# Linear stream of a fused attention and transformer kernel: biases by TensorE, maxima subtracted at eviction, all score products at once in four banks

## The reference

```python
vp = _ln(x, in_ln_w, in_ln_b) @ W_in
v, p = jnp.split(vp, 2, axis=-1)
q = softmax(to_heads(_ln(x, q_ln_w, q_ln_b) @ Wq + bq))
k = softmax(to_heads(_ln(x, k_ln_w, k_ln_b) @ Wk + bk))
k_prev = k shifted by one token
k = (1.0 - smear) * k + smear * k_prev          # smear by head
q, k = q / s, k / s                              # s by head
attn = jnp.tril(jnp.einsum('bhid,bhjd->bhij', q, k) * mask)   # mask: decay by head for 8 heads, ones for 8
norm = 1.0 / (attn.sum(axis=-1) + ATTN_EPS)
o = jnp.einsum('bhij,bhjd->bhid', attn * norm[..., None], v)
out = _ln(jax.nn.silu(p) * o @ W_out, out_ln_w, out_ln_b)
```

## Time and profile before

| | |
|---|---|
| median of 3 runs | 2380.59 us (2374.51 to 2381.43) |
| the profiled execution | 2383.1 us |
| its span | 2381.2 us |
| TensorE busy, products | 2168.9 us |
| TensorE busy, weight loads | 1867.6 us |
| VectorE busy | 1827.8 us |
| ScalarE busy | 1148.8 us |
| GpSimd busy | 934.9 us |
| TensorE's mean granted clock | 0.906 of 2.4 GHz |

### The profile page before, as it was taken

One profiled execution on the slowest core, in us unless ns is written; L12 is line 12 of the kernel. 1 busy time (PEld: TensorE's weight loads), 2 busy tenths in 40 slices (PEclk: granted clock), 3 DMA queues, 4 the chain that ended last, 5 costly groups with the idle time before them and its releaser, 6 DMA issues.

```text
span 2381.2 us, 48786 instructions
## 1 busy us (share of the span) xinstructions
PE 2168.9 (91%) x15282; PEld 1867.6 (78%) x15282; DVE 1827.8 (77%) x5354; ACT 1148.8 (48%) x2734; POOL 934.9 (39%) x941
## 2 busy tenths in 40 slices
PE   4889989999899989999899989989999999999997
PEld 3778877877787877877787877878888888888786
DVE  5667887778767787688767887777888888888885
ACT  2234443344334443344333443346677676776764
POOL 3334453345434453345433453343333333333331
PEclk8778998889978898899888998889999999999999
DMA  4000000000000000000000000012111111111110
GB/s 162 11 13 17 20 18 14 15 19 18 14 13 19 15 18 14 13 21 18 14 13 15 19 18 14 14 51 69 33 36 33 33 37 32 36 33 33 37 33 25
DMA packets 71792, 64.37 MB, mean 27 GB/s; under 512 B 12444, under 2 KB 64984, under 8 KB 71608
## 3 DMA queue, kind: packets, MB, share of 16 engines
q1 hardware_dynamic: 71736, 63.65, 8.9%
HBM read 38.45 MB, written 12.58 MB: 21 GB/s over the span
## 4 chain that ended last, share of the span: by engine, by line
PE 50%; DVE 30%; issue 13%; DMA 3%; ACT 1%; DVEq 1%; SPq 1%; POOL 1%; POOLq 0%; ACTq 0%
PE bank L1327 38%; PE bank L1332 7%; PE bank L1339 5%; DVE prob L940 4%; DVE prob L926 4%; DMA x_shift<-x 2%; DVE rot L1250 2%; DVE sq_sum L1196 2%; DVE qk_sum L1209 2%; DVE rot L1228 1%; DVE hid L1257 1%; DVE v_mix L1223 1%; DVE mix_work L982 1%; DVE h_n L1158 1%; DVE h_n L1156 1%
## 5 line engine op out<-in xcount | busy, mean ns | idle before, releaser
L1327 PE MATMUL bank<-hT_n,w_s 128*128 128x128 f32 x3072 | 389.6, 279 | 0.5 <-ACT hT_n L711 0.5
L1327 PEld LDWEIGHTS bank<-hT_n,w_s 128*128 128x128 f32 x3072 | 364.9, 193 | 15.2 <-issue 10.8
L1332 PE MATMUL bank<-wqkv_s,xT 128*128 128x512 f32 x1152 | 319.4, 413 | 24.0 <-DVE xT L1104 18.4
L741 ACT ACTIVATE prob<-prob,row_min 128x256 f32<-128x256 f32 x512 | 256.1, 503 | 63.8 <-DVE row_min L926 61.5
L1327 PE MATMUL bank<-w_s,hid 128*128 128x256 f32 x768 | 284.5, 489 | 0.2 <-DVE hid L1257 0.2
L1332 PEld LDWEIGHTS bank<-wqkv_s,xT 128*128 128x128 f32 x1152 | 207.8, 192 | 81.8 <-DVE xT L1104 27.1
L711 ACT ACTIVATE k_dec<-bank 128x512 f32<-128x512 f32 x32 | 19.1, 598 | 515.6 <-PE bank L1339 515.6
L940 DVE TENSOR_SCALAR prob<-prob,row_inv 128x256 f32<-128x256 f32 x512 | 224.3, 480 | 9.2 <-DVE row_inv L935 0.2
L926 DVE CUSTOM_DVE_ANT_0 prob<-bank,table,inv_norm 128x256 f32<-128x256 f32 x512 | 226.2, 478 | 2.7 <-issue 2.7
L633 POOL TENSOR_TENSOR rot_other<-raw,rot_t 128x256 f32<-128x256 f32 x256 | 186.5, 761 | 93.3 <-ACT raw L711 93.3
L596 POOL TENSOR_TENSOR inv_norm<-sq_clip,half_neg 128x16 f32<-128x16 f32 x64 | 188.7, 2948 | 63.6 <-DVE sq_clip L1199 63.6
(11 more groups left out here) (182 smaller groups left out, 4699.8 us busy)
## 6 DMA issues: line engine op xcount, KB each, us to landing
k_prev<-k_carry SPq DMA_DIRECT2D x32, 224.0 KB, 2.5
x_s<-in_L_attn_x SPq DMA_DIRECT2D x32, 128.0 KB, 2.1
rot_s<-in_rotary SPq DMA_DIRECT2D x64, 64.0 KB, 2.0
s_between_passes<-s_out SPq DMA_DIRECT2D x32, 128.0 KB, 1.7
x_between_layers<-x SPq DMA_DIRECT2D x32, 128.0 KB, 1.7
x_s<-x_between_layers SPq DMA_DIRECT2D x32, 128.0 KB, 2.0
xn<-x_between_layers SPq DMA_DIRECT2D x32, 128.0 KB, 2.1
s_out<-s_between_passes SPq DMA_DIRECT2D x32, 128.0 KB, 2.1
```

What stands on the lines that cost most here:

```text
L741: ins = act.activation(prob[:, h, :], prob[:, h, :], ACT.Exp, bias=row_min[:, c:c + 1], scale=-1.0, accum_out=row_sum[:, c:c + 1])
L1327: return pe.matmul(out, lhsT, rhs, start=first, stop=last)
L1332: ins = pe.matmul(out, halved(left[:, a]), halved(right[:, b]), start=first and n == 0, stop=last and n == 2)
```

## The change

- The biases of q, k and p are no longer added at eviction. `bias_rows` holds each bias as a high part in row 0 and a low part in row 32, and `pick` has ones in these rows; a first product of 64 rows puts the bias in the bank, and the linear products accumulate on it. v keeps its addition. Setup makes these tiles.
- `less_max`: DVE takes the maxima straight from the bank and subtracts them as it evicts, k first, then q. PE computes k ahead of q. ACT takes the exponential of k and of q by themselves, DVE sums by halves. POOL's subtraction goes.
- tanh reads the bank; the gate is one DVE product, (tanh + 1) times the bank. POOL's two products go.
- All four row groups of the scores are issued in one go, into `mix_bank[0]`, `mix_bank[1]`, `att_bank[0]` and `att_bank[2]`; DVE multiplies all four with the masks, one after the other, ahead of `low_turned` and `residual`. `out_projection` writes `att_bank[1]` in these iterations.
- Order: the key sum (kadd) comes ahead of the rotation products on DVE; the sums of squares (`norms`) come behind the gate; scores b1 come ahead of weighing b0, in all iterations; POOL makes `k_dec` ahead of the inverse norm; PE transposes k and q behind the transposes of b1; two of the second MLP matrix's products come ahead of the output loop, two within it, behind g = 1 and g = 3.

```diff
-        bias_mix = sb("bias_mix", [P, 4, ME])
+        bias_v = sb("bias_v", [P, ME])
+
+        bias_rows, bias_in = sb_halves("bias_rows", [P, 3, ME])
+        pick, pick_in = sb_halves("pick", [P, P])
...
+        score_bank = [mix_bank[0], mix_bank[1], att_bank[0], att_bank[2]]
...
+            pool.memset(pick_in[:, :], 0.0).then_inc(picked, 1)
...
+            pool.memset(pick_in[0:1, :], 1.0).then_inc(picked, 1)
...
-                if mix is not None:
-                    n = mix
-                    pool.wait_ge(mix_dve.sem, mix_dve.at("max", n))
-                    qk_h = qk.rearrange("p (h d) -> p h d", d=MD)
-                    pool.tensor_tensor(qk_h, qk_h, qk_max[:, :].unsqueeze(2).to_broadcast([P, 2 * MH, MD]),
-                                       ALU.subtract).then_inc(mix_pool.done("sub"), 1)
...
-                if proj is not None:
-                    u, p = proj, proj.parity
-                    pool.wait_ge(proj_dve.sem, proj_dve.at("clip", u))
-                    root(inv_norm[:, p, :], sq_clip[:, :], 2 * H).then_inc(proj_pool.done("inv"), 1)
-                if mix is not None:
-                    n = mix
-                    pool.wait_ge(mix_act.sem, mix_act.at("tanh", n))
-                    pool.tensor_tensor(gate[:, :], p_tanh, p_lin, ALU.mult).then_inc(mix_pool.done("gatep"), 1)
-                    pool.wait_ge(mix_pool.sem, mix_pool.at("gatep", n))
-                    pool.tensor_tensor(gate[:, :], gate[:, :], p_lin, ALU.add).then_inc(mix_pool.done("gate"), 1)
...
+                if proj is not None:
+                    u, p = proj, proj.parity
+                    pool.wait_ge(proj_dve.sem, proj_dve.at("clip", u))
+                    root(inv_norm[:, p, :], sq_clip[:, :], 2 * H).then_inc(proj_pool.done("inv"), 1)
+                if mix is not None:
+                    n = mix
...
+                    act.wait_ge(mix_dve.sem, mix_dve.at("ksub", mix))
+                    act.activation(qk[:, ME:2 * ME], qk[:, ME:2 * ME], ACT.Exp).then_inc(mix_act.done("kexp"), 1)
...
+                    act.wait_ge(mix_dve.sem, mix_dve.at("qsub", mix))
+                    act.activation(qk[:, 0:ME], qk[:, 0:ME], ACT.Exp).then_inc(mix_act.done("qexp"), 1)
...
-                    act.wait_ge(mix_pool.sem, mix_pool.at("sub", mix))
-                    act.activation(qk, qk, ACT.Exp).then_inc(mix_act.done("exp"), 1)
...
-                    act.wait_ge(mix_dve.sem, mix_dve.at("p", mix))
-                    act.activation(p_tanh, p_lin, ACT.Tanh, scale=0.5).then_inc(mix_act.done("tanh"), 1)
+                    act.wait_ge(mix_pe.sem, mix_pe.at("p", mix))
+                    act.activation(p_tanh, mix_bank[1][:, :], ACT.Tanh, scale=0.5).then_inc(mix_act.done("tanh"), 1)
...
-                b = mix_bank[r % 2][:, :].rearrange("p (g i) -> p g i", g=MG)
+                b = score_bank[r][:, :].rearrange("p (g i) -> p g i", g=MG)
...
+            def less_max(mix, name, b, at):
+
+                rows = qk_max[:, at * MH:(at + 1) * MH]
+                dve.wait_ge(mix_pe.sem, mix_pe.at(name, mix))
+                dve.tensor_reduce(rows, heads(b[:, :]), AX_X, ALU.max).then_inc(mix_dve.done(name + "max"), 1)
+                dve.wait_ge(mix_dve.sem, mix_dve.at(name + "max", mix))
+                dve.tensor_tensor(heads(qk[:, at * ME:(at + 1) * ME]), heads(b[:, :]),
+                                  rows.unsqueeze(2).to_broadcast([P, MH, MD]), ALU.subtract)\
+                   .then_inc(mix_dve.done(name + "sub"), 1)
+
+            def norms(u):
+
+                dve.wait_ge(proj_act.sem, proj_act.at("square", u))
+                dve.tensor_reduce(sq_sum[:, :], rot[:, :].rearrange("p (h d) -> p h d", d=HD), AX_X, ALU.add)\
+                   .then_inc(proj_dve.done("sqsum"), 1)
+                dve.wait_ge(proj_dve.sem, proj_dve.at("sqsum", u))
+                dve.tensor_scalar(sq_clip[:, :], sq_sum[:, :], 1e-24, None, ALU.max)\
+                   .then_inc(proj_dve.done("clip"), 1)
...
+            b_hi = prob[0:64, 0:6, :].rearrange("p h d -> p (h d)").rearrange("p (n e) -> p n e", n=3)
+            dve.tensor_copy(halved(b_hi), bias_in[0:64, :, :]).then_inc(setup_dve.done("bhi"), 1)
+            dve.wait_ge(setup_dve.sem, setup_dve.at("bhi", ONCE))
+            dve.tensor_tensor(halved(bias_rows[32:64, :, :]), bias_in[32:64, :, :], b_hi[32:64], ALU.subtract)\
+               .then_inc(setup_dve.done("blo"), 1)
+            dve.tensor_copy(halved(bias_rows[0:32, :, :]), b_hi[0:32]).then_inc(setup_dve.done("brow"), 1)
+            dve.wait_ge(picked, 3)
+            dve.tensor_copy(halved(pick[:, :]), pick_in[:, :]).then_inc(setup_dve.done("brow2"), 1)
...
+                if mix is not None:
+                    less_max(mix, "k", mix_bank[0], 1)
+                if a is not None:
                     weigh("a0", a)
                 if mix is not None:
-                    dve.wait_ge(mix_pe.sem, mix_pe.at("q", mix))
-                    dve.tensor_tensor(qk[:, 0:ME], mix_bank[0][:, :], bias_mix[:, 2, :], ALU.add)\
-                       .then_inc(mix_dve.done("q"), 1)
+                    less_max(mix, "q", mix_bank[1], 0)
                 if a is not None:
                     weigh("a1", a)
+                if mix is not None:
+                    dve.wait_ge(mix_act.sem, mix_act.at("kexp", mix))
+                    dve.tensor_reduce(qk_sum[:, MH:2 * MH], heads(qk[:, ME:2 * ME]), AX_X, ALU.add)\
+                       .then_inc(mix_dve.done("ksum"), 1)
+                    dve.wait_ge(mix_dve.sem, mix_dve.at("ksum", mix))
+                    dve.reciprocal(k_norm[:, :], qk_sum[:, MH:2 * MH]).then_inc(mix_dve.done("kinv"), 1)
+                    dve.wait_ge(mix_dve.sem, mix_dve.at("kinv", mix))
+                    dve.tensor_tensor(k_smear[:, :], k_norm[:, :], smear_s[:, :], ALU.mult)
+                    dve.tensor_tensor(k_keep[:, :], k_norm[:, :], keep_s[:, :], ALU.mult)\
+                       .then_inc(mix_dve.done("kw"), 1)
+                if a is not None:
+                    scores("b1", a, att_bank[0])
                     weigh("b0", a)
...
-                if mix is not None:
-                    dve.wait_ge(mix_pe.sem, mix_pe.at("k", mix))
-                    dve.tensor_tensor(qk[:, ME:2 * ME], mix_bank[1][:, :], bias_mix[:, 3, :], ALU.add)\
-                       .then_inc(mix_dve.done("k"), 1)
-                    dve.wait_ge(mix_dve.sem, mix_dve.at("k", mix))
-                    dve.tensor_reduce(qk_max[:, :], heads(qk), AX_X, ALU.max).then_inc(mix_dve.done("max"), 1)
...
-                    dve.wait_ge(mix_pe.sem, mix_pe.at("p", mix))
-                    dve.tensor_tensor(p_lin, mix_bank[1][:, :], bias_mix[:, 1, :], ALU.add)\
-                       .then_inc(mix_dve.done("p"), 1)
-                if mix is not None:
-                    dve.wait_ge(mix_act.sem, mix_act.at("exp", mix))
-                    dve.tensor_reduce(qk_sum[:, :], heads(qk), AX_X, ALU.add).then_inc(mix_dve.done("sum"), 1)
...
+                if u is not None and mix is None:
+                    norms(u)
+                if mix is not None:
+                    dve.wait_ge(mix_act.sem, mix_act.at("qexp", mix))
+                    dve.tensor_reduce(qk_sum[:, 0:MH], heads(qk[:, 0:ME]), AX_X, ALU.add)\
+                       .then_inc(mix_dve.done("qsum"), 1)
+                    dve.wait_ge(mix_dve.sem, mix_dve.at("qsum", mix))
                     dve.tensor_tensor(q_eps[:, :], qk_sum[:, 0:MH], head_eps[:, :], ALU.mult)\
                        .then_inc(mix_dve.done("qeps"), 1)
-                if a is not None:
+                    dve.wait_ge(mix_pe.sem, mix_pe.at("v", mix))
+                    dve.tensor_tensor(v_mix[:, :, 0:MD], heads(mix_bank[0][:, :]), heads(bias_v[:, :]),
+                                      ALU.add).then_inc(mix_dve.done("v"), 1)
+                if a is not None and mix is not None:
                     weigh("b1", a)
                 if mix is not None:
-                    dve.wait_ge(mix_pe.sem, mix_pe.at("v", mix))
-                    dve.tensor_tensor(v_mix[:, :, 0:MD], heads(mix_bank[0][:, :]), heads(bias_mix[:, 0, :]),
-                                      ALU.add).then_inc(mix_dve.done("v"), 1)
+
+                    dve.wait_ge(mix_act.sem, mix_act.at("tanh", mix))
+                    dve.scalar_tensor_tensor(gate[:, :], p_tanh, 1.0, mix_bank[1][:, :], ALU.add, ALU.mult)\
+                       .then_inc(mix_dve.done("gate"), 1)
+                if u is not None and mix is not None:
+                    norms(u)
+                if mix is not None:
+                    dve.wait_ge(mix_pool.sem, mix_pool.at("kkeep", mix))
+                    dve.wait_ge(k_shifted, 48 * mix.number() + 32)
+                    dve.tensor_tensor(qk[:, ME:2 * ME], qk[:, ME:2 * ME], k_prev[:, :], ALU.add)\
+                       .then_inc(mix_dve.done("kadd"), 1)
+                if a is not None and mix is None:
+                    weigh("b1", a)
...
```

(61 more changed lines are left out.)

104 lines of the change are left out of this document (40 added, 64 removed).

## The result

The changed kernel takes 2232.66 us (median of 4 runs, 2230.43 to 2235.16), the kernel before 2381.01 (4 runs): ratio 0.938, 95% interval 0.9358 to 0.9403. That is 148 us faster; the forecast was 209, 2172 us. The range, 2135 to 2335, holds the time; the forecast's own part of it, 2140 to 2221, does not.

What follows compares the result with a forecast made beforehand. VectorE, then TensorE set the time, with 13.38 us of TensorE work nearly all at half clock. Saving 7.2 us in 27 iterations (194) plus 20 elsewhere, less 5 for setup, gives 209 less: 2172 us, range 2135 to 2335.

Steps and rivals of the forecast that it cites:

- the forecast's own part: Range of the main forecast alone, from periods of 40.3 to 43.3 us: 2140 to 2221 us; chance 0.60.
- The stall and the clock in the loop: TensorE's 1.69 us stall ahead of the output loop goes, and the clock stays at 2.4 GHz through the loop.
- The rival that thin products alone bring the clock down: Output loop stays at low clock even without the stall: period 46.65, 2321 us; chance 0.21.
- The transposes: Rival: clock falls at the transposes around the key-sum wait, rises at the output projection; period 45.1, 2270 us; chance 0.09.
- When the key sum comes: Key sum on VectorE ends at 738.3 in place of about 742.1, 3.8 us earlier.
- The seven new instructions: VectorE's added maxima, subtractions, half sums and gate product over 512 elements: 0.64 us each on average, 4.4 in all.
- The root: GpSimd's inverse root, behind the key decay, ends 5.2 us behind the key sum; output difference 0.9 us later than before.
- The wait before the projection: TensorE waits 1 to 1.5 us before the output projection; the clock falls in some iterations, 0.4 us on average.
- From the loop to W_out: Output loop's start to the projection of W_out takes 7.95 us, against 15.47 in the profiled iteration.
- The sum: Period: 31.45 to the loop, plus 7.95, 1.69 and 0.4, gives 41.5 us against 48.68; in all 209 us less.
- the last piece: From the projection of W_out to the next iteration's start: 1.69 us.
- The setup: Three added VectorE instructions over 1536 elements ahead of the first iteration: 4 to 7.5 us, taken as 5.

Runs made afterwards that it cites:

- e2: Kernel before with only its score part changed: four banks, all 32 products at once, decays in one row, projection into the other bank; 2141.88 us.
- e8: e1 plus one idle reduction over 2048 elements on VectorE ahead of the last decay of the scores; 2215.74 us.
- e10: e8 with the second layer's products back in the output loop, one behind each group, none ahead of it; 2346.23 us.
- e3: Changed kernel with the scores in two pairs through the two mix banks again; 2317.94 us.
- e1: Changed kernel with one step moved on GpSimd: inverse root ahead of the key decay; 2110.18 us.
- e7: e1 with the scaling of the next window's normalised input moved behind both state additions on VectorE; 2098.91 us.
- e5: e1 plus two idle reductions over 1024 elements on VectorE ahead of the last decay of the scores; 2273.51 us.
- e6: e1 plus two idle reductions over 1024 elements on VectorE ahead of the second half's output difference; 2235.12 us.
- e9: e1 plus one idle reduction over 2048 elements on VectorE ahead of the second half's output difference; 2242.4 us.

## Why the prediction was right, and by how much it was off

**The stall and the clock in the loop: right.** From iteration 2 on the loop starts without idle time (0.09 us at most), and its clock is 1.00 but for the last 0.15 to 0.44 us of the low stretch in four iterations. That this is where the gain is made is shown from both sides: the four banks alone bring 234 us (e2 against the kernel before, 2376.1 us beside it), and a stall put back brings the low clock back, in 14 of 29 iterations (e8) or 23 of 29 (e10). The rival that thin products alone bring the clock down fell. But the cause as I put it, "the stall of 1.69 us directly ahead of thin products", is not sufficient: e8 has 1.64 and escapes in half of its iterations, where the kernel before never did. What that had besides were the second layer's products in the loop (e10 has them there, with a longer stall, and falls in 23 of 29) and the second pair of thin score products just ahead of the stall (no run has these with such a stall; in e3 full products stand between). Which of them makes up the rest of the way to every iteration stays open, and so does why one stall of 1.64 is followed by a fall and the next is not.

**The transposes: the rival fell.** The eight transposes of k and q at 849.62 had a clock of 1.00 in every iteration from 2 on, as the window 741.70 to 745.10 had suggested.

**When the key sum comes: right.** Forecast offset 20.24 from the iteration's start, measured 20.54. It is free of GpSimd (0.69 us). The seven new instructions took 0.67 to 0.69 each, 0.6 without the overlap of neighbours, where I had taken 0.64.

**The root: mis-sized, the failed step.** I had the root start when the key decay ends and take its 2.96 us, with nothing for the second rotation product. The decay ended 2.04 us behind the key sum (forecast 2.23). But the second rotation product had begun inside it, at 850.88, and ran until 852.62; the root, started at 851.50, took 3.88 us, 2.76 from that product's end. So it ended at offset 26.4 and the output difference at 29.0, each 1.0 later than forecast. In e1 it took 3.31 us: it started 0.15 behind the start of the key sum and ended some 2.8 us behind that instruction's end, with both rotation products beside it, each at 1.2. Both rows fit one reading: the root waits for the VectorE instruction that is under way, and then neither holds up the other. So the exclusion for the whole length, which the prediction took for such a pair and which its gate product and key sum bear out, does not hold for the root.

**The wait before the projection: seen, but under-priced.** I expected 1 to 1.5 us there and a fall "in some iterations", 0.4 on average. It was 2.55 us, and VectorE was idle 2.80 us ahead of the key scaling where I had 1 to 2; the fall came in 23 of 27 iterations at 1.7 each: 1.5 on average. e1 is the test: no wait, no low stretch. This and the root's late end are one cause, the order of two instructions on GpSimd, which I had priced at 0.9 us against the kernel before and which was worth 3.9.

**From the loop to W_out: 0.9 too short.** Forecast 7.95, measured 8.88 to 8.95 in nearly every iteration. 0.77 of it is TensorE's wait for VectorE's state additions. In the kernel before, at the low clock, this wait was 0 to 0.25 us (765.92 has none): TensorE then took longer than VectorE, and halving its time uncovered the wait. e7 removes half of it.

**The sum.** Period: 41.5 forecast; loop start without a low stretch at offset 31.85 in place of 31.45, +0.4; loop to W_out +0.9; the low stretches +1.1; the last piece 1.62 in place of 1.69, -0.1. That gives 43.8; measured 43.85. In 27 iterations these 2.35 us make 63 us. The setup cost 4.6 us (first transposes at 33.94, 29.33 before) against 5 forecast, the layer-1 part 1.5 against 0, and the first three and last two iterations gave 28 where I had 20. Together 153 in the span for the 209 forecast. Two sums of the prediction are off by little: 746.1 and 2.7 make 748.8 for the last decay, not 749.1, and the terms from the root's end to the output difference make 746.0; neither moves the loop's start by more than 0.1.

## What to carry to other kernels

A stall ahead of thin products costs more than its length, since the clock of what follows goes with it, so price a wait by what stands behind it: where the clock fell, 2.0 to 2.6 us ahead of the full products of the projection cost 1.6 to 1.7 more, 1.6 to 2.3 us ahead of the thin loop mostly 4 to 6 more (2.7 to 2.9 where the stretch was short). It is a price with a share of iterations, from 3 of 17 to all, which no row here foretells. Where a change makes one engine's stretch much shorter, look for the waits that its slowness had covered, and walk through each re-ordered queue again with the new times: swapping two steps on the least busy engine was worth 122 us here, nearly four times what all of the change but the four banks brings (32).

## What was not expected of the hardware

The 32 score products took 0.98 us of weight loads where 16 took 0.97: products 32 rows deep in all four row groups went out at twice the rate of those in two. With e3's two pairs, 16 again take 0.97.

Added instructions on VectorE had a price that no row of busy time shows. With two more in each half of its loop the instruction queue's packets went from 26 to 86 and VectorE stood still for 2.8 to 3.6 us in each of 12 passes (e5, e6); with one more this happened in e9 (3.8 us a pass), and in e8, with one instruction more in the same loop too, it did not. What sets it apart stays open. A row "issue" of some 3 us on an otherwise fed engine, together with a grown instruction queue whose packets fall into it, is how it shows in these traces.
